# Finer steps and a new merge order for a two-stream attention kernel

## The reference

```python
mod = (silu(c) @ wmod)            # per sample: sa, ca, ga, sb, cb, gb
h = layernorm(x) * (1 + ca) + sa
x = x + ga * attn(h)              # 16 samples of 512 x 128, 16 heads of 8, causal, latent k and v
h = layernorm(x) * (1 + cb) + sb
x = x + gb * ffn(h)               # 2 layers, below
# one layer: h = shift_token(x); q, k, v = split(h @ wqkv)         8 heads of 64
#   q = l2norm(q) * qs; k = l2norm(k) * ks; rotary with xpos scale on both
#   o = softmax over a window of 64 and the 64 before it; x = x + o @ wo
#   h = layernorm(shift_token(x)) * lg + lb; a, g = split(h @ w1 + b1)
#   x = x + (a * gelu(g)) @ w2 + b2
```

## Time and profile before

| | us |
|---|---|
| median of 3 runs | 2433.9 |
| lowest and highest run | 2421.71, 2438.56 |
| the profiled execution: device time | 2427.62 |
| the profiled execution: span on the core | 2425.8 |
| PE busy in it | 2183.1 |
| DVE, ACT, POOL busy | 1646.6, 1587.9, 563.6 |

### The profile page before, as it was taken

One profiled execution on the slowest core, in us unless ns is written; L12 is line 12 of the kernel. 1 busy time (PEld: TensorE's weight loads), 2 busy tenths in 40 slices (PEclk: granted clock), 3 DMA queues, 4 the chain that ended last, 5 costly groups with the idle time before them and its releaser, 6 DMA issues. The chain is left out here.

```text
span 2425.8 us, 52449 instructions
## 1 busy us (share of the span) xinstructions
PE 2183.1 (90%) x21002; PEld 1383.2 (57%) x21002; DVE 1646.6 (68%) x2617; ACT 1587.9 (65%) x3047; POOL 563.6 (23%) x528
## 2 busy tenths in 40 slices
PE   3599899998999899998999989999899989999897
PEld 2455656556565466655565555655656546666454
DVE  2465877676866768667776676776776676866664
ACT  1267766767667676676666776667766767667664
POOL 2012330222302412024210243012330231202410
PEclk9799999999999999999999999999999999999998
DMA  3300132001320012100220012300131001320001
GB/s 100 61 9 17 32 58 43 2 17 37 58 39 17 14 35 54 31 17 16 51 55 12 17 32 46 50 6 17 37 53 43 17 1 37 52 36 18 16 17 25
DMA packets 62521, 78.67 MB, mean 32 GB/s; under 512 B 9266, under 2 KB 57004, under 8 KB 59948
## 3 DMA queue, kind: packets, MB, share of 16 engines
q1 hardware_dynamic: 62284, 75.33, 16.0%
HBM read 11.40 MB, written 4.19 MB: 6 GB/s over the span
## 5 line engine op out<-in xcount | busy, mean ns | idle before, releaser
L872 DVE TENSOR_REDUCE nm<-ps 128x2 f32<-128x768 f32 (+3 forms) x384 | 388.4, 1042 | 121.6 <-PE ps L562 114.8
L1009 POOL TENSOR_TENSOR pr<-pr 128x1024 f32<-128x1024 f32 x128 | 302.2, 2361 | 678.9 <-DVE pr L910 678.9
L805 ACT ACTIVATE pr<-ps,wb,inv 128x128 f32<-128x128 f32 x1024 | 370.6, 490 | 97.8 <-DVE wb L927 97.8
L505 PE MATMUL ps<-cf,pr 128*128 128x128 f32 x2048 | 284.6, 279 | 100.4 <-POOL pr L1019 69.0
L505 PEld LDWEIGHTS ps<-cf,pr 128*128 128x128 f32 x2048 | 225.7, 141 | 161.9 <-POOL pr L1019 81.7
L762 ACT ACTIVATE pr<-ps 128x896 f32<-128x896 f32 x256 | 233.4, 921 | 70.3 <-PE ps L580 67.0
L903 DVE TENSOR_TENSOR pr<-ps,rot 128x1024 f32<-128x1024 f32 x128 | 156.5, 1223 | 149.2 <-ACT pr L777 143.7
L777 ACT ACTIVATE pr<-ps 128x1024 f32<-128x1024 f32 x128 | 131.1, 1025 | 143.8 <-PE ps L628 81.4
L580 PE MATMUL ps<-Q,K 128*128 128x512 bf16 (+3 forms) x1024 | 223.7, 299 | 0.0
L561 PE MATMUL ps<-K,Q 128*128 128x128 bf16 x1024 | 196.6, 222 | 28.2 <-DMA K<-Kf 25.3
L921 DVE TENSOR_REDUCE wm<-ps 128x8 f32<-128x1024 f32 x128 | 156.7, 1224 | 69.0 <-PE ps L659 68.0
(11 more groups left out here) (151 smaller groups left out, 4453.3 us busy)
## 6 DMA issues: line engine op xcount, KB each, us to landing
pr<-V SPq DMA_DIRECT2D x32, 520.0 KB, 4.7
Q<-Kf SPq DMA_DIRECT2D x224, 64.0 KB
K<-Kf SPq DMA_DIRECT2D x224, 64.0 KB
pr<-V SPq DMA_DIRECT2D x32, 390.0 KB, 6.2
xn<-in_L_attn_x SPq DMA_DIRECT2D x16, 256.0 KB, 2.8
out<-hT SPq DMA_DIRECT2D x16, 256.0 KB, 2.2
Q<-in_c_edge SPq DMA_DIRECT2D x32, 64.0 KB
Q<-mT SPq DMA_DIRECT2D x128, 4.0 KB
```

The lines of the kernel that those rows point to most:

```text
L505: mm = pe.transpose(dst[:, t * P:(t + 1) * P], src(t), ident)
L805: ins = act.activation(P2[s][:, 2 * (p % 2) + r, o:o + P], bank[:, r * T + o:r * T + o + P], ACT.Exp, scale=inv[s][:, t, h:h + 1], bias=wb ...
L872: dve.tensor_reduce(nm[s][:, qt, h0:h0 + n], src, AX_X, ALU.max, negate=True).then_inc(nm_r[s], 1)
L1009: pool.tensor_tensor(t1[s][t % 3], t1[s][t % 3], t2[s], ALU.add).then_inc(sum_r[s], 1)
```

## The change

`steps()` writes smaller steps. `spread` gives its DVE part to a new step `scale`. `proj` becomes two steps (q, k), on SP too. `score` gives the tail tiles to `tail` (8 for a sample), with a semaphore of its own, `exb_r`. `qkv` becomes `qkv` (q and k on PE, squares on ACT), `rotate` (DVE and POOL parts) and `v` (PE and ACT). `heads` becomes `qheads` and `kheads`. `wscore` keeps its PE and DVE parts and gives ACT's to `wexp` (one for each head); `pturn` and `wctx` become one step for each head. The instructions, their shapes and their tiles are the same; a few waits on semaphores that one step had before are now in both halves (the two waits for `hs` in `v`, the wait for the edge rows in `tail`).

A new table `PLACES` permutes the 198 groups of steps of one sample before they are merged, and `ALL` and `FIRST_BANKS` are new:

```diff
-            out += [("qkv", l, t)] * (t < NT) + [("norm", l, t - 1)] * (1 <= t <= NT) + [("heads", l, t - 2)] * (t >= 2)
+            out += [("qkv", l, t), ("rotate", l, t), ("v", l, t)] * (t < NT) + [("norm", l, t - 1)] * (1 <= t <= NT)
+            out += [("qheads", l, t - 2), ("kheads", l, t - 2)] * (t >= 2)
         for p in range(NP2 + 3):
-            out += [("wscore", l, p)] * (p < NP2) + [("wctx", l, p - 2)] * (2 <= p <= NP2 + 1)
-            out += [("pturn", l, p - 1)] * (1 <= p <= NP2) + [("wturn", l, p - 3)] * (p >= 3)
-        out += [("wout", l), ("center", 2 + l), ("spread", 2 + l)]
+            out += [("wscore", l, p), ("wexp", l, p, 0), ("wexp", l, p, 1)] * (p < NP2)
+            out += [("wctx", l, p - 2, r) for r in range(2)] * (2 <= p <= NP2 + 1)
+            out += [("pturn", l, p - 1, r) for r in range(2)] * (1 <= p <= NP2) + [("wturn", l, p - 3)] * (p >= 3)
+        out += [("wout", l), ("center", 2 + l), ("spread", 2 + l), ("scale", 2 + l)]
...
+PLACES = [
+    0, 1, 2, 3, 4, 6, 7, 5, 8, 9, 10, 11, 19, 12, 13, 14, 15, 20, 21, 22, 16, 23, 17, 24, 25, 27, 18, 26, 28, 29,
...
-    rest = [iter([[(s + S2 * (k - back), name) for back, name in names[i:j]] for k in range(B // S2 + 1)
-                  for i, j in zip(firsts, firsts[1:])]) for s in range(S2)]
+    groups = [names[i:j] for i, j in zip(firsts, firsts[1:])]
+    rest = [iter([[(s + S2 * (k - back), name) for back, name in groups[i]] for k in range(B // S2 + 1) for i in PLACES])
+            for s in range(S2)]
...
                     elif kind == "proj":
-                        sp.wait_ge(*hi_r.at(b, 1))
-                        for r in range(2):
+                        i, = a
+                        sp.wait_ge(*hi_r.at(b, i + 1))
+                        for r in range(2 * (i == 0)):
```

More of the change, by code:

```diff
@@ L54 @@
 SPREADS = 16 * 2 * (2 * SLOTS + 1)
-SHIFTS = {("spread", 1): 0, ("wout", 0): 1, ("down", 0): 2, ("wout", 1): 3}
+SHIFTS = {("scale", 1): 0, ("wout", 0): 1, ("down", 0): 2, ("wout", 1): 3}
 def steps():
@@ L88, in steps @@
-    return between + [(0, name) for name in out[:cut]]
[L94 to L99, removed]
+    cut = out.index(("pturn", DEPTH - 1, NP2 - 1, 1)) + 1
@@ new lines, in steps @@
+    first = {("pturn", DEPTH - 1, NP2 - 1, 1): [("load",)], ("wctx", DEPTH - 1, NP2 - 1, 0): [("center", 0)],
+             ("wturn", DEPTH - 1, NP2 - 2): [("spread", 0), ("scale", 0)],
+             ("wturn", DEPTH - 1, NP2 - 1): [("proj", 0), ("proj", 1)]}
+    between = [(0, name) for name in first[out[cut - 1]]]
+    for last in out[cut:]:
+        between += [(1, last)] + [(0, name) for name in first.get(last, [])]
+    return between + [(0, name) for name in out[:cut]]
+PLACES = [
[8 rows of a table added]
+]
+ALL = ("00001040d162aa0c0004674e994edb77b7fd1e3a9140b3d121101000d735bb66706411e7ffdbd34b088214108e9f7ee69a4aafffeffb"
+       "4e8ca200012674ec94edb77b7fd363a8940d5d121101000d6d5af2db60411e7ffddc74b084214110eb79fe69a62afffeffb4e8ca2000"
+       "246b4e994edb77b7fe2e3a9140b5d111101000d735b73a760411d7ffdbcb26888212110e76ff671664afffeffb4e8ca2000246b4e955"
+       "6db77b7fe1e3a9140b5d111200800d6b5af2e760409e7ffddd347044218110eaf7ee99652afffeffb4e8ca2000126b4ea94edb77b7fe"
+       "1e3a9140add121201000d6b5f536760411d7ffdbd34b084214110eaeff6b164cafffeffb4e8ca200024674ea94edb77b7fd1e3a9140b"
+       "5d111100800d6b9af8dd60409d7ffdbd34b084214104eaeff6a96466fffeffb4e8ca2000246b4ea94edb77b7fe1e3a5140b5d1208808"
+       "00d6b9e796b50409d7ffdf54a6884214108ecf7eea9652afffeffb4e8ca200028674e994edb77b7fe2e3a5140b5d120881000d6b9af5"
+       "5b50209d7ffddd347084228211c9efee71668a7fffff72ea6208000e8a6da94ecfcfb7797b5a4c40abc8a20500015bb1ba97750908ae"
+       "fffbd49b042c21fffffffffffff")
@@ L111, in merged @@
             out += [(b, name) for b, name in group if 0 <= b < B]
-    assert len(out) == B * len(names)
+    assert len(out) == B * len(names) and sorted(PLACES) == list(range(len(groups)))
     return out
 ORDER = merged()
[L119 to L144, removed]
@@ new lines, in step @@
+                        pe.wait_ge(*pt_r.at(b, 2 * n + r + 1))
+                        bank, full = banks.take(pe, (b, "pv", l, p, r), [tok_r.at(b, 2 * n + r + 1)])
+                        for j in range(NT):
+                            for half, val in enumerate((VB, V2)):
+                                q0 = j * P + half * D2
+                                mm = pe.matmul(bank[D2 * half:D2 * half + D2, j * (D2 + 1):(j + 1) * (D2 + 1)],
+                                               PT[s][:, (2 * n + r) % 3, q0:q0 + D2], val[s][:, j, 2 * p + r, :],
+                                               start=True, stop=True, skip_group_check=True)
```

243 lines of the change are left out of this document (137 added, 106 removed), and 7 rows, old and new, of the table PLACES.

## The result

The changed kernel takes 2401.3 us (median of four runs, 2395.7 to 2414.6) where the kernel before, run beside it, takes 2431.7: a ratio of 0.9885 [0.9853, 0.9917]. It is faster by 1.2%, about 28 us, where 48 were forecast. The profiled execution took 2405.4 us with a span of 2403.6, against 2425.8 before: 22.2 us less.

A forecast was written before the change was run, and what follows sets the result against it. PE's queue was taken to set the time, with about 175 us of its idle time winnable. The terms -105 - 10 - 5 + 26 + 13 + 12 + 21 = -48 took 2427.6 to 2380 us, range 2322 to 2432.

The forecast's parts named there:

- The k transposes: PE's waits for POOL's scaling of k: longer PE distance removes 54 us of 69.0, bounds 38 and 69.
- The smaller waits: PE waits at `pturn` -20, `center` to `spread` -12, `ctx` to `turn` -10, `rows1` and `hid` -9; stated together as -31.
- All named waits: The k transposes and the smaller waits on PE together: -105 us.
- the +21 set aside for what comes back: PE reaches next waits sooner with ACT and DVE no faster: a fifth of the 105 returns, +21 us (0 to +60).
- What comes with a wait: Removed PE waits also remove exposed transpose time, -10 us (0 to -20), and clock dips, -5 us.
- The DMAs: PE waits for SP's 28 copies: `score8` +26 us (0 to +50), first `max` of even samples +13 (0 to +30).
- Other new waits: Shorter distances from `wturn` to `wout`, `wctx` to `wturn` and `join` to `out`: +12 us, bounds 0 and +30.
- Rival 1: Waits return as POOL, DVE and ACT limit `qkv` and window stages: 2429 us at worst, some 2415 otherwise; chance 0.19.
- Rival 2: SP's 28 copies decide, traffic ending at +28 us behind `proj`: slower by 17 us, 2445; chance 0.11.
- Rival 3: Copies are in time, edge rows overtake them, little comes back: 2290 to 2325 us, 2315 taken; chance 0.14.
- The signs named: Right if POOL L1019 falls to 20 or less, ACT L805 below 10, and new DMA waits total 15 to 40 us.

The follow-up runs named there:

- the second measurement: The changed kernel run again with no edit, beside the kernel before: 2412.0 us, ratio 0.9926.
- half_add: Changed kernel with POOL's addition on 512 of its 1024 columns (k half of the rotation not added, output not the reference's): 2397.4 us, 0.9842 of the kernel before.
- edge_early: Changed kernel with SP issuing the even sample's edge rows after 22 of the odd sample's 28 copies: 2371.6 us, 0.9764 of the kernel before.
- late_score8: Changed kernel with three `hid` steps of the other stream put ahead of the even sample's `score8`, except in the first sample: 0.9789 of the kernel before.
- early_late8: Changed kernel with both the early edge-row issue on SP and three `hid` steps ahead of `score8`: 2370.9 us, 0.9759 of the kernel before.
- early_half: Changed kernel with the early edge-row issue and POOL adding 512 of 1024 columns (output not the reference's): 2365.8 us, 0.9720 of the kernel before.

## Why the prediction was right, and where its sum was not

The direction, the order of magnitude and the two kinds of new wait came out as forecast; the gain is little over half of the forecast one (28 us, and 18 in the second measurement, of 48). Step by step, as waits of PE by step, before to after:

- **The k transposes are the step that failed.** The prediction's words are: "3.2 more than covers 2.8: all 37.7 go. ... Together -54, bounds -38 and -69". Measured: 70.1 to 43.6, that is -26.5, outside the bounds. The first tile of layer 1 went from 37.7 to 20.8, tile 1 of layer 0 rose from 10.3 to 17.2; only tile 2 of each layer did as forecast (12.4 to 2.7 and 2.7 to 0). The step took one tile's chain on POOL and held it against PE's distance, as though POOL were free when its input came. The timeline of POOL and PE in one such wait of the changed kernel shows what it left out, two additions back to back (one of each stream) before the scaling starts:

```profile
1110.93 4.69 POOL L1042 TENSOR_TENSOR pr<-pr 128x1024 f32<-128x1024 f32 x2
...
1115.71 0.27 POOL L1047 TENSOR_SCALAR inv<-inv 128x16 f32<-128x16 f32 x1
...
1116.13 1.04 POOL L1052 TENSOR_TENSOR pr<-pr,inv 128x512 f32<-128x512 f32 x1
```

and the windows around it, PE's busy time first and POOL's fifth:

```profile
1107.00:1111.00 4.00, 2.32 (x15) 1.52 (x14) 4.00 (x5) 3.29 (x9) 3.53 (x6) 1.00 0.00 0
1111.00:1115.00 4.00, 3.81 (x19) 2.05 (x17) 2.84 (x5) 3.10 (x8) 4.00 (x2) 1.00 0.00 0
1115.00:1119.00 4.00, 2.08 (x8) 1.07 (x8) 3.18 (x4) 2.48 (x7) 3.53 (x6) 1.00 0.02 6
```

  POOL is busy for 11.1 of 12 us and PE for 8.2. An engine at 23% of the span is here the bound, since both streams are in their `qkv` steps at once. But this case is only half of the row. Of the 40 waits, 15 (20.8 us) end a stretch in which POOL ran two to four additions without a pause, busy for over 90% of the last 8 us. Another 24 (22.5 us, among them all of tile 1 of layer 0) look like this one, 8 us earlier:

```profile
1105.52 2.36 POOL L1042 TENSOR_TENSOR pr<-pr 128x1024 f32<-128x1024 f32 x1 [1.08 <-DVE pr L946]
...
1108.39 1.04 POOL L1052 TENSOR_TENSOR pr<-pr,inv 128x512 f32<-128x512 f32 x1
...
1109.48 0.77 PE L525 MATMUL ps<-cf,pr 128*128 128x128 f32 x5 [1.68 <-POOL pr L1052]
```

  POOL stood idle here for DVE's products of the next tile, and k's `norm` stood behind that tile's addition in its queue, as in the earlier trace rows; addition and scaling then took 3.9 us. The new list freed only tile 2 of this order. So the chain that PE's distance had to cover begins with POOL's backlog or with DVE's product for the next tile, and not with the tile's own input, and it moves along with the list. That POOL's work is in both kinds is shown by a run: half_add, which takes 1.2 us a tile off POOL, takes the row to 18.3, and the two runs with another order on POOL only move the wait. The prediction had the number (3.7 us a tile) and used it for "more than nothing" coming back. ACT's part of `norm` matters little: ahead of waits of 2.9 of the 43.6 us POOL had last stood idle for ACT, ahead of the others for DVE. A faster DVE there was not tested.
- **The smaller waits.** The prediction gives "These four: -31", but its own terms (-20, -12, -10 and -9) make -51, and -51 is what its sum of -105 holds. `pturn` -13.0 for -20, `spread` -15.7 for -12, `turn` -12.4 for -10: close. `rows1` and `hid` together came to +6 for -9: `rows1` gave 2, but `hid` rose by 8.2, since the first of layer 0 went from 0 to 11.8. That half_add cuts `hid` to 5.8 shows that this wait hangs on POOL too, by way of a list that moves as one. All named waits: -61.5, not -105, and the +21 set aside for what comes back is about half of the 44 that are missing.
- **What comes with a wait.** PE's busy time fell by 9.6 us beside the missing records, for the -15 of exposure and clock. How much of it is the clock's is not shown apart; the mean granted clock went from 0.979 to 0.981.
- **The DMAs.** At `score8` +42.2 for +26. In the seven samples of mid-run, which the step priced, it was 29.7 (6.5, 4.1, 0.9, 5.9, 0.7, 5.2, 6.4), about as forecast. The other 12.5 are the first sample's, which the step left out ("in seven samples"): the term was under-sized by a case that hadn't been looked at, not by its mechanism. At the first `max` of even samples 14.0 for +13. The step had PE arrive 21.7 us behind `proj` and the rows at 26 in the mean; PE arrived at 21.5 and went on at 22.2 to 28.0, 25.8 in the mean. Edge_early and late_score8 show the mechanism from both sides.
- **Other new waits** +12: `qheads` 3.9, `wturn` 3.8 and the other `score` steps 1.2 are new, 9 together; but 12 in `tail`, `wctx`, `wscore`, `join` and `ctx` and 4 at the start went. With small changes elsewhere it came to -7. No term of the prediction had these gains, so 19 us of the result are luck.
- **The sum as measured.** Named waits -61.5 for -84 (the -105 with the +21 that comes back), the DMAs +56 for +39, the rest -7 for +12, PE's work -9.6 for -15: -22 for -48. Three terms were too favourable by 45 us, and the one that was too careful gave 19 back.
- **The rivals.** Rival 1 (2415 to 2429, POOL the limit in the `qkv` stages) was right in its mechanism, though even its 37.7 was too much, and the smaller gains saved the time from it; the result lies between it and the 2380 of the sum, near the upper end of the 2345 to 2405 that the forecast was given. Rival 2 needed a mean end of the traffic of +27.5, and even PE's restart lay at 25.8. Rival 3, that the edge rows overtake the copies, is excluded as the kernel stands (42.2 us of waits), and even through ACT's queue they overtook none that was issued before them.
- **The signs named.** PE L579 and L561 (now L530 and L587) waited for DMA in mid-run and at the first `score8`, 56 us for the 15 to 40 named. L1019 fell to 43.6 and ACT L805 to 16.5, each short of its mark (20 and 10). POOL's row above 40 was the sign of rival 1, and it came.

The gains that were real were partly returned at the copies: their end hangs on `proj` and on their own traffic, so what PE saves between `proj` and `score8` is waited for there (12 us more in half_add). Putting that right (edge_early, 0.9764, or early_late8, 0.9759) gives 2371 us, below both kernels, without an instruction more.

## What to carry to other kernels

A wait of PE is one of distance only if the engine waited for is free when its input comes: look at that engine's busy time in windows of some 10 us around the wait, with all streams in it, and at what stands ahead of the answer in its queue and what that waits for, before counting a longer distance as a gain. When steps are moved, price every wait whose end is fixed by something other than PE (a batch of DMAs here) for each sample, the first and last too, since it takes back whatever is gained ahead of it. A small transfer that an engine soon needs should not be issued behind a large batch of which nothing is yet needed, on the same queue or on another: in this kernel the moment of issue decided, and with the new list an earlier one gave 40 us where the list alone had given 18 to 28. Count the records of an engine before comparing two busy times of it.

## What the runs showed of the hardware

- Small DMAs behind a large batch came in the order of issue, whatever the queue. On SP's queue, issued at 402.67 behind 28 copies, two of 4 KB released PE at 411.37, and traffic at 72 GB/s lasted until 410. Through ACT's queue, issued at 968.21 when SP had issued 20 copies, they moved from 974.54 on, when 20 copies had moved. The Trainium skill, page "DMA: Bandwidth & Descriptors", section "Queues, rings and completion order", says that completion is not first in, first out per issuing engine. These rows show no such overtaking on SP's queue, and none from ACT's. The same page (section "Issuing engines are not separate DMA queues") has all issuing engines share the same DMA engines, so that a second one only saves the time of issuing. The run through ACT's queue agrees: the rows were issued some 6 us earlier behind `proj`, and that was the gain. Why they wait for the copies ahead of them on another queue is open.
- The same 28 copies of 64 KB ran at 72 and 75 GB/s in windows of one pair of samples and at 97 in another (the windows above), and their traffic ended 26.6 and 21.3 us behind `proj`. An estimate of a wait on them needs that spread, not its mean.
- A trace can lack records of one kind and not of another: 105 to 119 matmuls of `score` are missing in most runs here, none in the kernel before and in early_half, and each leaves an idle gap of some 52 ns.
- One POOL addition of 128x1024 takes 2.36 us, and two back to back 4.69.
